# Block-diagonal attention keys: written by two masked activations on ScalarE instead of one copy and four DMAs; projections three steps ahead instead of four; the output's bias added on GpSimd

## The reference

```python
q = xh @ Wq; k = xh @ Wk; v = xh @ Wv            # xh = groupnorm(x), channels last
# windows of 8x8 pixels: token (r, c) of all 16 windows attend to each other, 8 heads of 28
q2 = q2 * scale
sim = einsum('bmhid,bmhjd->bmhij', q2, k2) + pos_emb      # 16 x 16 per head and position
attn = softmax(sim, axis=-1)
o = einsum('bmhij,bmhjd->bmhid', attn, v2)
o = o @ Wo + bo
x = x + o
```

## Time and profile before

| | us |
|---|---|
| median of 3 runs (lowest, highest) | 3675.77 (3672.93, 3676.39) |
| the profiled execution's own time | 3674.84 |
| its span | 3672.9 |
| PE, DVE, ACT, POOL busy | 3608.4, 3032.9, 2940.0, 2045.4 |
| granted TensorE clock | 1.00 in all but the last slice |

### The profile page before, as it was taken

The page is one execution under the profiler, slowest core; times in us unless marked ns, Lnnn a source line. Parts: engine busy times, 40 slices in busy tenths (PEclk is TensorE's granted clock), DMA queues, the critical chain, the costliest instruction groups (busy, mean ns, idle before and its releaser), DMA issues.

```text
span 3672.9 us, 167555 instructions
## 1 busy us (share of the span) xinstructions
PE 3608.4 (98%) x67842; PEld 2625.2 (71%) x67842; DVE 3032.9 (83%) x5028; ACT 2940.0 (80%) x5377; POOL 2045.4 (56%) x3334
## 2 busy tenths in 40 slices
PE   5999999999999999999999999999999999999998
PEld 3777777777777777777777777777777777777776
DVE  6888888888888888888888888888888888888876
ACT  6888888888888888888888888888888888888874
POOL 4555555555555555555555555555555555555553
PEclk9999999999999999999999999999999999999999
DMA  4555555555555555555555555555555555555544
GB/s 95 139 144 136 146 144 142 137 145 143 141 138 150 142 137 143 145 143 137 143 146 144 136 145 144 144 134 145 143 145 135 145 142 145 136 146 143 141 126 117
DMA packets 252111, 513.67 MB, mean 140 GB/s; under 512 B 62672, under 2 KB 63120, under 8 KB 251536
## 3 DMA queue, kind: packets, MB, share of 16 engines
q1 hardware_dynamic: 250000, 504.35, 52.4%
q10 hardware_dynamic: 1536, 0.07, 0.0%
HBM read 118.31 MB, written 117.44 MB: 64 GB/s over the span
## 4 chain that ended last, share of the span: by engine, by line
PE 87%; issue 5%; POOL 3%; DVE 2%; ACT 1%; DMA 0%; POOLq 0%; SPq 0%; DVEq 0%; ACTq 0%
PE ps_out L327 18%; PE ps_q L327 16%; PE ps_k L327 16%; PE ps_v L327 14%; PE ps_o L370 13%; PE ps_s L358 10%; POOL sc L724 1%; ACT xn L484 1%; POOL xlo L732 1%; POOL newton L706 1%; DVE part L622 0%; POOL sc L737 0%; PE ps_tot L423 0%; DVE sc L651 0%; DVE pt_f L664 0%
## 5 line engine op out<-in xcount | busy, mean ns | idle before, releaser
L724 POOL TENSOR_TENSOR sc<-sc,mx 128x512 f32<-128x512 f32 x512 | 536.5, 1048 | 876.3 <-DVE mx L658 876.3
L484 ACT ACTIVATE xn<-x_sb,norm_add,norm_mul 112x128 f32<-112x128 f32 x2048 | 1016.7, 599 | 5.0 <-POOL norm_add L717 3.1
L737 POOL TENSOR_TENSOR sc<-sc,rs 128x512 f32<-128x512 f32 x512 | 536.4, 1048 | 421.7 <-DVE rs L678 421.6
L327 PE MATMUL ps_out<-ohi,wo_s 128*112 128x256 f16 x4096 | 720.8, 278 | 3.1 <-DVE x_sb L634 3.1
L646 DVE TENSOR_TENSOR olo<-ps_o,ohi 128x512 f16<-128x512 f32 x512 | 353.8, 691 | 350.0 <-ACT ohi L526 338.8
L511 ACT ACTIVATE sc<-sc 128x512 f32<-128x512 f32 x512 | 323.3, 632 | 396.3 <-POOL sc L724 396.1
L327 PE MATMUL ps_q<-xhi,wqk 112*128 112x512 f16 x2048 | 611.2, 380 | 12.5 <-POOL xlo L732 9.9
L327 PE MATMUL ps_k<-xhi,wqk 112*128 112x512 f16 x2048 | 609.7, 379 | 0.6 <-ACT q_sb L501 0.6
L370 PE MATMUL ps_o<-p_bd,v_sb 128*32 128x128 f32 x16384 | 553.5, 276 | 9.1 <-DMA p_bd<-pt_f 6.6
L327 PE MATMUL ps_v<-wv_s,xhi 112*128 112x224 f16 x4096 | 560.6, 259 | 0.0
L732 POOL TENSOR_TENSOR xlo<-xn,xhi 112x1024 f16<-112x1024 f32 x256 | 547.3, 2138 | 13.1 <-ACT xhi L495 13.1
(11 more groups left out here) (76 smaller groups left out, 5827.6 us busy)
## 6 DMA issues: line engine op xcount, KB each, us to landing
k_bd<-k_cut SPq DMA_DIRECT2D x1024, 128.0 KB
p_bd<-pt_f SPq DMA_DIRECT2D x2048, 64.0 KB, 2.5
x_sb<-in_x SPq DMA_DIRECT2D x256, 448.0 KB, 4.5
out_y<-x_sb SPq DMA_DIRECT2D x256, 448.0 KB, 3.5
k_cut<-in_L_conv_Wq SPq DMA_DIRECT2D x2, 98.0 KB
k_cut<-in_L_conv_Wk SPq DMA_DIRECT2D x2, 98.0 KB
k_cut<-in_L_conv_Wv SPq DMA_DIRECT2D x2, 98.0 KB
pt_f<-in_L_conv_Wo SPq DMA_DIRECT2D x8, 24.5 KB
```

The costliest lines, as they stand in the source:

```text
L327: last = nc.tensor.matmul(dst, w_parts(a, ch), x_parts(c, ch), start=(n == 0), stop=(n == 3 * chunks - 1))
L484: nc.scalar.activation(xn[:, b % 2, :, c4, :, :, nw].rearrange("p r c q -> p q r c"), x_sb[:, b % XBUFS].rearrange("p ch (nh r w) -> p (ch ...
L724: nc.gpsimd.tensor_tensor(rows, rows, mx[:, t % 2].unsqueeze(2).broadcast_to(by_row), ALU.subtract).then_inc(shifted, 1)
L737: nc.gpsimd.tensor_tensor(rows, rows, rs[:, t % 2].unsqueeze(2).broadcast_to(by_row), ALU.mult).then_inc(probs, 1)
```

## The change

- ACT writes the keys itself: in place of one Copy of `ps_k` to `k_cut` there are two Identity activations of the same 128x512, one to `k_bd[..., 0]` and one to `k_bd[..., 1]`, each with `scale` = a column of a mask `head_mask` (1 on the partitions of even heads in one, of odd heads in the other). The four DMAs per half, `k_cut`, the zeroing of `k_bd` and the semaphores `k_placed` go. `k_kept` counts two per step, and PE waits for it where it waited for the placed keys.
- All leads shrink by one (`PROJ_LEAD` 4 to 3, and so on), the lags stay. The kernel has one step fewer in all, and the work of an image before attention stands one step later relative to attention: `xhi` and `xlo` in even steps, and so on.
- `add_bias` moves from ACT to the end of POOL's step, as a tensor_tensor add with `bo` broadcast along 1024 columns, again in two of four steps (t % 4 == 1 and 3).

```diff
-LOAD_LEAD, SUM_LEAD, RSQ_LEAD, TOT_LEAD, STAT_LEAD = 15, 14, 13, 12, 11
-NORM_LEAD, SPLIT_LEAD, PROJ_LEAD = 9, 5, 4
+LOAD_LEAD, SUM_LEAD, RSQ_LEAD, TOT_LEAD, STAT_LEAD = 14, 13, 12, 11, 10
+NORM_LEAD, SPLIT_LEAD, PROJ_LEAD = 8, 4, 3
...
 # SP
-                u = t + PROJ_LEAD
-                if is_step(u) and u % 2 == 1:
-                    h = u // 2
-                    per_step(sp, k_kept, u, i)
-                    for hd in range(HPG):
-                        p = slice(hd * DP, hd * DP + DP)
-                        sp.dma_start(k_bd[p, h % 2, :, hd % 2, :], k_cut[p, h % 2]).then_inc(k_placed[h % 2], 16)
...
 # PE
-                            keys_placed(pe, g // 2, i)
+                            per_step(pe, k_kept, g + 1, i, 2)
...
-                    per_step(pe, k_kept, u - 1, i)
+                    per_step(pe, k_kept, u - 1, i, 2)
...
 # ACT
-                    nc.scalar.activation(k_cut[:, h % 2, hg], ps_qk[1][:, :], ACT.Copy).then_inc(k_kept, 1)
+                    nc.scalar.activation(k_bd[:, h % 2, hg, 0], ps_qk[1][:, :], ACT.Identity,
+                                         scale=head_mask[:, 0:1]).then_inc(k_kept, 1)
+                    nc.scalar.activation(k_bd[:, h % 2, hg, 1], ps_qk[1][:, :], ACT.Identity,
+                                         scale=head_mask[:, 1:2]).then_inc(k_kept, 1)
                 normalize(t, 1, i)
-                add_bias(image_at(t, SPLIT_LEAD - 1), 0, i)
-                add_bias(image_at(t, SPLIT_LEAD - 2), 1, i)
...
 # DVE, once
-            nc.vector.memset(k_bd[:, 0].rearrange("p b c d -> p (b c d)"), 0.0).then_inc(pads_zeroed, 1)
+            for hd in range(HPG):
+                for n in range(2):
+                    nc.vector.memset(head_mask[hd * DP:hd * DP + DP, n:n + 1], float(hd % 2 == n)).then_inc(zeroed, 1)
...
 # POOL
+            def add_bias(b, ch, i):
+                if b is None:
+                    return
+                per_image(pool, normed, b, i, G)
+                wait(pool, summed, 2 * CH * b + 2 * CH, i, 2 * CH * XBUFS)
+                nc.gpsimd.tensor_tensor(x_sb[:, b % XBUFS, ch], x_sb[:, b % XBUFS, ch],
+                                        bo_sb[:, ch:ch + 1].broadcast_to((CP, TOK)), ALU.add).then_inc(bias_added, 1)
...
                 root(image_at(t, STAT_LEAD), 0, i)
+                add_bias(image_at(t, SPLIT_LEAD - 1), 0, i)
+                add_bias(image_at(t, SPLIT_LEAD - 3), 1, i)
```

More of the change, by code:

```diff
@@ L92, in build @@
         q_sb = sb("q_sb", [128, QBUFS, HG, HTOK])
-        k_cut = sb("k_cut", [128, 2, HG, HTOK])
         k_bd = sb("k_bd", [128, 2, HG, 2, HTOK])
@@ L107, in build @@
         wo_s = sb("wo_s", [128, 2, HG, C], F16)
-        wqk_f = k_cut[0:CP].rearrange("p a b c -> p (a b c)").rearrange("p (ch c) -> p ch c", ch=CH)[:, :, 0:512]
-        wv_f = k_cut[0:CP].rearrange("p a b c -> p (a b c)").rearrange("p (ch c) -> p ch c", ch=CH)[:, :, 512:512 + C]
+        wqk_f = k_bd[0:CP, 0].rearrange("p a b c -> p (a b c)").rearrange("p (ch c) -> p ch c", ch=CH)[:, :, 0:512]
+        wv_f = k_bd[0:CP, 0].rearrange("p a b c -> p (a b c)").rearrange("p (ch c) -> p ch c", ch=CH)[:, :, 512:512 + C]
         wo_f = pt_f[:].rearrange("p a c -> p (a c)").rearrange("p (hg c) -> p hg c", hg=HG)[:, :, 0:C]
@@ L125, in build @@
         ones = sb("ones", [128, 128])
+        head_mask = sb("head_mask", [128, 2])
         ps_qk = (ps("ps_q", [128, HTOK]), ps("ps_k", [128, HTOK]))
@@ L166, in build @@
         v_kept = sem("v_kept")
-        k_placed = [sem(f"k_placed{n}") for n in range(2)]
         p_placed = [sem(f"p_placed{n}") for n in range(2)]
@@ L185, in build @@
         ROOT_OPS = 4 * NEWTON
-        N_ZEROED = 8
+        N_ZEROED = 8 + 2 * HPG
         def wait(eng, s, n, i, per_round):
@@ L216, in per_image @@
             wait(eng, s, each * (b + 1), i, each * PERIOD // 4)
-        def keys_placed(eng, h, i):
-            each = 16 * HPG
-            wait(eng, k_placed[h % 2], each * (h // 2 + 1), i, each * PERIOD // 4)
         def probs_placed(eng, g, i):
@@ L431, in weights_split @@
             def weights_split():
-                pe.wait_ge(pads_zeroed, 4)
+                pe.wait_ge(pads_zeroed, 2)
                 pe.wait_ge(w_hi, 3)
@@ L436, in _ @@
             pe.wait_ge(zeroed, N_ZEROED)
-            rounds(pe, step, before_11=bound_weights, before_4=weights_split)
+            rounds(pe, step, before_10=bound_weights, before_3=weights_split)
         @block.scalar
@@ L454, in weights_split @@
                 act.wait_ge(w_lo, 3)
-                act.wait_ge(pads_zeroed, 4)
+                act.wait_ge(pads_zeroed, 2)
             def square(b, ch, i):
@@ L462, in square @@
                 nc.scalar.activation(sq[:, ch, :], x_sb[:, b % XBUFS, ch], ACT.Square).then_inc(squared, 1)
[L464 to L471, removed]
             def normalize(t, n, i):
@@ L526, in step @@
                     nc.scalar.activation(ohi[:, g % 2], in_x_order(ps_o[:, :]), ACT.Copy).then_inc(o_hi, 1)
-            rounds(act, step, before_12=load_positions, before_4=weights_split)
+            rounds(act, step, before_11=load_positions, before_3=weights_split)
         @block.vector
@@ L572, in split_weights @@
                     nc.vector.tensor_copy(hi[:, 0], full).then_inc(w_hi, 1)
-                nc.vector.memset(k_bd[:, 1].rearrange("p b c d -> p (b c d)"), 0.0).then_inc(pads_zeroed, 1)
                 dve.wait_ge(w_hi, 3)
@@ L678, in step @@
                     nc.vector.reciprocal(rs[:, t % 2], sm[:, t % 2]).then_inc(inverted, 1)
-            rounds(dve, step, before_10=split_weights)
+            rounds(dve, step, before_9=split_weights)
         @block.gpsimd
@@ L740, in step, with small_there @@
                 root(image_at(t, STAT_LEAD), 0, i)
+                add_bias(image_at(t, SPLIT_LEAD - 1), 0, i)
+                add_bias(image_at(t, SPLIT_LEAD - 3), 1, i)
+            def small_there():
+                pool.wait_ge(small_loaded, 16 * N_SMALL)
             pool.wait_ge(zeroed, N_ZEROED)
-            rounds(pool, step)
+            rounds(pool, step, before_3=small_there)
 N_WEIGHTS = 2 * CH + CH + HG * HPG
```

## The result

The changed kernel takes 3715.3 us (median of 5 runs, 3715.25 to 3716.23) against 3675.77 (5 runs, 3672.93 to 3676.39): ratio 1.011, 95% interval 1.0097 to 1.0122. It is 39.5 us slower. The forecast was 3736, range 3700 to 3762.

The account below looks back on a forecast made before the run. The prediction took a ring through ACT, DVE and POOL, level with PE before, to set the pace alone afterwards: 3672.9 + 64 - 5 + 3 - 1 = 3733.9 as span, 3736 us with 1.9 around it; range 3700 to 3762.

Parts of the forecast that it names:

- The ring bounds as much as PE does: Chain exp, `ohi`, `olo`, L651, maximum, POOL's subtraction, next exp takes 28.18 us per four steps; PE needs 28.09.
- Bias off ACT: Bias add stood between exp and `ohi`; removal shortens the ring by 0.98 us in two steps of four, to 26.22.
- Second key write: Second key write on ACT, between exp and `ohi`, lengthens the ring by 0.62 us in every step, 0.48 to 0.79.
- The new ring: 26.22 + 4 x 0.62 = 28.70 us per four steps, above PE's 28.09: +64 us over 496 steps.
- Bias on POOL: Add at the end of POOL's step fits before L724 with 0.1 us to spare: 0, upper bound +37 us.
- DMAs off SP: 1024 key DMAs go; nothing waited on their landing in the steady part: 0.
- Keys late (C): Rival: PE stalls at the scores in odd steps, 26 us per 0.1 us, from 3762 us up; chance 0.04.
- Leads: One step less of filling -5 us, last projection one step later at the end +3, PE nearer the ring -1.
- Rival A: PE stays the bound if the second write costs 0.48 us, operand free: 3661 to 3672, say 3668; chance 0.14.
- PE's idle time at 3 to 4%, ended by xlo or L651: Sign of being right: PE's idle time rises from 2% to 3 to 4%, ended by `xlo` or L651.
- PE still without waits while the time grows: Sign named for the prediction being wrong as a whole, beside a ring that has become shorter elsewhere.

Follow-up runs that it names:

- e3: Kernel before with only the bias add moved to the end of POOL's step, keys still by DMA, old leads: 3668.6 us.
- e11: Kernel before with the bias add left on ACT but moved behind `ohi`, nothing else changed: 3667.8 us.
- e4: Changed kernel with the bias add back on ACT at its old place: 3962.0 us.
- e1: Changed kernel with its second key write moved behind `ohi` in ACT's step, same work in another order: 3676.9 us.
- e8: Changed kernel with POOL's bias add cut to 16 of 1024 columns: 3713.6 us.
- e6: Changed kernel with the second key write behind `ohi` and the old leads of 15 to 4: 3664.9 us.
- e5: Changed kernel with the old leads of 15 to 4: 3719.6 us.
- e2: Changed kernel with both key writes as plain copies without the mask: 3676.6 us.
- e7: Changed kernel with the second key write behind `ohi` and the loop started at step 13 instead of 12: 3670.4 us.
- e9: Changed kernel with the second key write behind `ohi` and the loop started at step 14 instead of 12: 3663.3 us.
- e10: Changed kernel with the second key write behind `ohi` and the loop started at step 16 instead of 12: 3661.6 us.

## Why the prediction was right, step by step

- *The ring bounds as much as PE does.* Right. e3 and e11 show it on the kernel before, and e4 meets the time that the ring gives to 0.1%.
- *Bias off ACT: -0.98 in two steps of four.* Right: e4 puts it back and costs 3962.0 - 3715.3 = 246.7 us, that is 1.99 for each of 124 times four steps.
- *Second key write: +0.62 per step.* Right in kind: e1 shows that its place on the ring is what costs. Measured 1.13 - 0.53 = 0.60. I charged the first write most of an operand; it pays 0.02. This term alone is 4 x 0.02 x 124 = 10 us too long.
- *The new ring: 28.70 per four steps.* Measured 4 x 7.141 = 28.57. Besides the 0.08 of the key writes the base of 26.22 was 0.05 too long (28.57 - 4 x 0.60 = 26.17). Part of that is visible in the kernel before: its 28.18 holds what the steps around the branch add, and in the middle of a turn four steps took 28.14. Together 0.13 x 124 = 16 us of the 19.5 by which the span was overestimated.
- *Bias on POOL: 0.* Right (e8), with the duration 12% under the one taken from `xlo` (1.89 for 2.14), so POOL got 473 us busier and not 540.
- *DMAs off SP: 0.* No run isolates it. In the changed kernel the key DMAs are gone and the ring's pace is accounted for by ACT's instructions, so it is near 0 there, argued and not shown alone. Where PE bounds, e6 differs from e3 by the key DMAs and the writes together, and they are worth 3.7 us (3664.9 for 3668.6).
- *Keys late (C).* No wait of PE for a key write appears. As such a wait could hide in busy time, e1 is the better witness: its second write comes later still, and PE keeps its own pace of 28.1 per four steps in the middle of a turn.
- *Leads: -5, +3, -1.* Measured -6.0 and +0.1. The start was mis-sized by 1 and the end by 2, 3 us in all. e5 gives the leads alone: 5.7 us won at the start and 2.3 lost at the end, 3.4 for the 3 of the forecast (the rest of its 4.3 lies in the steps between). So +2 was right for what the leads do to the end, and something else in the change took 2.3 us off it, which was not looked into.
- *Rival A* fails at its own threshold of 0.49 per step; e2 removes the mask, comes to 0.48 and lands at 3676.6. So A had the operand wrong. Its time for the case, 3661 to 3672, was 5 us too low as well: PE's branch lasts 2.15 us in e2, and the steps around it add 0.84 us in each of 20 turns, which A did not have.
- *PE's idle time at 3 to 4%, ended by xlo or L651.* Wrong. It is 76.4 us, 2.1%, for 64.5 before; the growth is in issue (16.4 us for 3.2), and the largest part is still two waits of `ps_tot` for POOL at the start (23.1). Read by the letter, this is nearly the sign that the prediction named for being wrong as a whole, "PE still without waits while the time grows". The sign was badly chosen, since the page counts most of PE's waiting as busy; e1 and e2 show that the ring is the cause all the same.
- *PE's branch.* Not in the prediction. It went from 0.69 to 2.12 us and cost nothing only because the ring was slower than PE. Where the ring came out below PE, as in e1, the time was 3676.9, and the prediction has 3661 to 3672 for a kernel bound by PE. That the forecast did not need this term is luck.

## What to carry to other kernels

Before work is moved between engines, look for a ring of links each of which is waited for in nearly every step, and price an instruction by whether it stands on the ring; busy shares don't tell. An instruction nobody on the ring waits for goes behind the one that is waited for: here that is one moved line, worth 38 us. And in a long unrolled loop whose pace TensorE sets try a few starting points: one constant moved 15 us in e1, and nothing in the changed kernel, where the ring set the pace.

## What the runs showed that I had not expected

PE's backward branch took 0.36 to 2.15 us by kernel (medians; the last of the 20, which leaves the loop, 0.09), while the other engines' took 0.04 to 0.09. In e1, e7, e9 and e10, all bound by PE, it followed the step at which the loop starts (12: 2.02, 13: 1.08, 14: 0.45, 16: 0.36), and the time followed it. e6 breaks the series with 0.36 at 12 and the old leads, and the cause stays open. A GpSimd add of 112x1024 with a broadcast operand took 1.89 us, the subtraction of two full f32 and f16 operands 2.14.
